# A fused Mamba, attention and expert kernel: query and key split into bfloat16 parts on TensorE and ScalarE instead of VectorE and ScalarE

## What is computed

```
x = x + mamba(group_norm(x))        # 256 inner channels, 16 states, 32 time steps
t = t + relu(attention(layer_norm(t)) @ proj_w + proj_b)
      attention: 8 heads of 16 channels over 800 tokens,
      softmax(q k^T * 128**-0.5) v, queries and keys kept at float32 precision
t = t + layer_norm(experts(layer_norm(t)) + layer_norm(t)) * gamma + beta    # top 2 of 8, per sample
```

## Time and profile before

| | |
|---|---|
| median of 3 runs | 1722.59 us (1722.4 to 1724.98) |
| profiled execution, span from first to last instruction | 1723.2 us |
| PE busy | 1238.6 us (72%) |
| DVE busy | 1338.4 us (78%) |
| ACT busy | 1110.6 us (64%) |
| POOL busy | 701.9 us (41%) |
| mean granted TensorE clock | 0.833 of full speed |

### The profile page before, as it was taken

One profiled execution on the slowest core, in us unless ns is written; L12 is line 12 of the kernel. 1 busy time (PEld: TensorE's weight loads), 2 busy tenths in 40 slices (PEclk: granted clock), 3 DMA queues, 4 the chain that ended last, 5 costly groups with the idle time before them and its releaser, 6 DMA issues. The chain is left out here.

```text
span 1723.2 us, 22121 instructions
## 1 busy us (share of the span) xinstructions
PE 1238.6 (72%) x7264; PEld 550.1 (32%) x7264; DVE 1338.4 (78%) x2280; ACT 1110.6 (64%) x2041; POOL 701.9 (41%) x399
## 2 busy tenths in 40 slices
PE   5124588868887688777886888588848873884994
PEld 3001432243224322432243224332323232322683
DVE  4898789888988889788979997899778972602465
ACT  4332767777776778677967686769676863682430
POOL 3464245524562356235623562346333641000265
PEclk9556788977898889878996899689968996896997
DMA  2540534145414641372228131824063404001562
GB/s 65 174 138 29 190 70 155 38 154 135 154 33 151 144 144 39 128 171 99 85 67 228 61 127 42 209 88 144 18 183 79 164 20 84 32 1 38 163 182 70
DMA packets 94023, 185.11 MB, mean 107 GB/s; under 512 B 15512, under 2 KB 48564, under 8 KB 93908
## 3 DMA queue, kind: packets, MB, share of 16 engines
q1 hardware_dynamic: 92500, 180.41, 35.2%
q0 software_dynamic: 1408, 3.29, 0.6%
HBM read 146.47 MB, written 36.86 MB: 106 GB/s over the span
## 5 line engine op out<-in xcount | busy, mean ns | idle before, releaser
L1274 DVE TENSOR_TENSOR_SCAN hst<-dA,PS 128x800 f32<-128x800 f32 x256 | 466.2, 1821 | 38.5 <-ACT dA L939 5.6
L1001 ACT ACTIVATE probs<-PS 128x400 f32<-128x400 f32 x800 | 343.0, 533 | 61.7 <-PE PS L1573 61.6
L939 ACT ACTIVATE dA<-dt_rep,a_sb 128x775 f32<-128x775 f32 x256 | 244.7, 959 | 78.6 <-DVE hst L1274 53.4
L1573 PE MATMUL PS<-q_stack,k_stack 99*128 99x400 bf16 (+1 forms) x896 | 238.5, 356 | 76.8 <-ACT probs L1001 51.0
L1269 DVE TENSOR_TENSOR PS<-u_rep,b_rep 128x800 f32<-128x800 f32 x256 | 267.6, 1045 | 14.1 <-DMA u_rep<-u_dram 2.3
L991 ACT ACTIVATE probs<-PS 128x400 f32<-128x400 f32 x400 | 200.4, 503 | 107.6 <-PE PS L1540 90.3
L1294 DVE CUSTOM_DVE_ANT_0 probs<-PS,probs 128x400 f32<-128x400 f32 x400 | 220.4, 574 | 41.6 <-issue 29.0
L796 POOL TENSOR_TENSOR sp_l<-hst,c_rep 128x800 f32<-128x800 f32 x72 | 135.6, 1883 | 196.2 <-DVE PS L1269 196.1
L1558 PE MATMUL PS<-probs,v_ext 128*32 128x400 f32 (+1 forms) x1792 | 206.9, 540 | 5.6 <-ACT probs L1001 5.6
L796 POOL TENSOR_TENSOR dt_sb<-hst,c_rep 128x800 f32<-128x800 f32 x72 | 135.7, 1884 | 110.8 <-DVE PS L1269 78.5
L1539 PE MATMUL PS<-k_stack,q_stack 96*128 96x400 bf16 (+1 forms) x448 | 152.0, 375 | 39.9 <-DVE k_neg L1253 37.5
(11 more groups left out here) (225 smaller groups left out, 2110.0 us busy)
## 6 DMA issues: line engine op xcount, KB each, us to landing
b_rep<-b_dram SPq DMA_DIRECT2D x64, 400.0 KB, 4.4
c_rep<-c_dram SPq DMA_DIRECT2D x64, 400.0 KB, 4.0
dt_rep<-dt_dram SPq DMA_DIRECT2D x64, 400.0 KB, 6.4
u_rep<-u_dram SPq DMA_DIRECT2D x64, 400.0 KB, 6.5
q_stack<-parts_dram SPq DMA_DIRECT2D x96, 100.0 KB, 4.3
k_stack<-parts_dram SPq DMA_DIRECT2D x96, 100.0 KB, 5.3
dt_dram<-dt_sb SPq DMA_DIRECT2D x16, 400.0 KB, 3.4
u_dram<-sp_l SPq DMA_DIRECT2D x16, 400.0 KB, 3.8
```

The source lines that it names most:

```text
L939: nc.scalar.activation(dA[:, i % NDA, :].rearrange("p (j t) -> p j t", t=T)[:, :, 1:T], dt_rep[:, gi, :].rearrange("p (j t) -> p j t", t=T ...
L1001: nc.scalar.activation(probs[:, j % NPROB, :], bank(4 + j % 3, HALF), ACT.Exp, scale=ATT_SCALE).then_inc(probs_ready.sem, 1)
L1274: nc.vector.tensor_tensor_scan(hst[:, i % 2, :], dA[:, i % NDA, :], dbu, 0.0, ALU.mult, ALU.add).then_inc(scan_done.sem, 1)
L1573: last = nc.tensor.matmul(bank(4 + j % 3, HALF)[strip], k_stack[:, h, kt * P:kt * P + strip.stop - strip.start], q_stack[:, h, q0:q0 + HAL ...
```

## The change

- **The split.** q and k stay in PSUM. ScalarE rounds what is there to a bfloat16 part; TensorE multiplies the part by a negated identity and accumulates onto the same PSUM banks, so that the remainder stands there; this is done twice, and ScalarE rounds three times for q and three times for k (before: two each, and VectorE did the four subtractions). The exponential of the Mamba half now runs ahead of the first rounding.
- **Negated keys.** The k projection uses a negated weight for the tokens 0 to 399. So k_stack holds the first 400 keys negated, k_neg and its two VectorE instructions per sample are gone, and TensorE waits for the stacks themselves. The first-half scores come out negated, so the maximum now subtracts them from the Relu, with the operands in the other order.
- **Signs.** The exponential's scale is negative for key tiles 0 to 2, positive for 4 to 6, and for key tile 3, which has both kinds of keys, a value per partition read from SBUF. The rows of ones in k_stack are -1 for the first half.
- **The step ahead of a maximum** (`tile_seen`) is gone: the waits stand directly before the maximum.
- At the start a negated weight (w_k_neg), a negated identity and the scale tile are made, and TensorE waits for the first of these before its first projection.

```diff
@@ -451,6 +451,11 @@
+        def unit_scale(i):
+
+            kt = unit(i)[1]
+            return (-ATT_SCALE if (kt + 1) * P <= HALF else ATT_SCALE if kt * P >= HALF else score_scale[:, 0:1])
+
         def group_of(i):
@@ -745,7 +750,10 @@
                 pool_order.after(pool, 0, nc.gpsimd.memset(v_ext[:, :, :, :], 1.0))
-                nc.gpsimd.memset(k_stack[KST:KST + 3, :, :], 1.0).then_inc(pads_set, 1)
+                pool_order.after(pool, 0, nc.gpsimd.memset(score_scale[:, :], ATT_SCALE))
+                pool_order.after(pool, 0, nc.gpsimd.memset(score_scale[0:HALF % P, :], -ATT_SCALE))
+                pool_order.after(pool, 0, nc.gpsimd.memset(k_stack[KST:KST + 3, :, 0:HALF], -1.0))
+                nc.gpsimd.memset(k_stack[KST:KST + 3, :, HALF:TOK], 1.0).then_inc(pads_set, 1)
                 pool.wait_ge(pads_set, 1)
@@ -962,15 +970,20 @@
                         if i == LOW_AT:
-                            act.wait_ge(q_up.sem, q_up.at(n, 1))
-                            nc.scalar.copy(q_part[:, 0, :], wide(4)).then_inc(qk_first.sem, 1)
                             if m is not None:
                                 exp_of(m, 1)
+                            act.wait_ge(q_up.sem, q_up.at(n, 1))
+                            nc.scalar.copy(q_part[:, 0, :], wide(4)).then_inc(qk_part.sem, 1)
                             act.wait_ge(k_up.sem, k_up.at(n, 1))
-                            nc.scalar.copy(k_part[:, 0, :], wide(6)).then_inc(qk_first.sem, 1)
-                            for i_part, (part, rest) in enumerate(((q_part, part_rest[:, :]), (k_part, sp_e[:, 0, :]))):
-                                act.wait_ge(qk_rest.sem, qk_rest.at(n, i_part + 1))
-                                nc.scalar.copy(part[:, 1, :], rest).then_inc(qk_second.sem, 1)
+                            nc.scalar.copy(k_part[:, 0, :], wide(6)).then_inc(qk_part.sem, 1)
+                            act.wait_ge(qk_rest.sem, qk_rest.at(n, 1))
+                            nc.scalar.copy(q_part[:, 1, :], wide(4)).then_inc(qk_part.sem, 1)
+                            act.wait_ge(qk_rest.sem, qk_rest.at(n, 2))
+                            nc.scalar.copy(k_part[:, 1, :], wide(6)).then_inc(qk_part.sem, 1)
+                            act.wait_ge(qk_rest.sem, qk_rest.at(n, 3))
+                            nc.scalar.copy(q_part[:, 2, :], wide(4)).then_inc(qk_parts.sem, 1)
+                            act.wait_ge(qk_rest.sem, qk_rest.at(n, 4))
+                            nc.scalar.copy(k_part[:, 2, :], wide(6)).then_inc(qk_parts.sem, 1)
                         if n > 0 and i == LOW_AT + 1:
@@ -999,7 +1012,7 @@
                             nc.scalar.activation(probs[:, j % NPROB, :], bank(4 + j % 3, HALF), ACT.Exp,
-                                                 scale=ATT_SCALE).then_inc(probs_ready.sem, 1)
+                                                 scale=unit_scale(j)).then_inc(probs_ready.sem, 1)
                             for acc in range(3):
@@ -1105,6 +1119,7 @@
                 dve.wait_ge(weights_in, NW[0])
+                nc.vector.tensor_scalar(w_k_neg[:, :], w_qkv_sb[:, C:2 * C], -1.0, None, ALU.mult).then_inc(w_k_turned, 1)
@@ -1236,26 +1251,7 @@
-                def rests():
-
-                    for i, (part, b, rest) in enumerate(((q_part, 4, part_rest[:, :]), (k_part, 6, sp_e[:, 0, :]))):
-                        dve.wait_ge(qk_first.sem, qk_first.at(n, i + 1))
-                        nc.vector.tensor_tensor(rest, wide(b), part[:, 0, :], ALU.subtract).then_inc(qk_rest.sem, 1)
-
-                def low_parts():
-
-                    for i, (part, rest) in enumerate(((q_part, part_rest[:, :]), (k_part, sp_e[:, 0, :]))):
-                        dve.wait_ge(qk_second.sem, qk_second.at(n, i + 1))
-                        nc.vector.tensor_tensor(part[:, 2, :], rest, part[:, 1, :], ALU.subtract).then_inc(qk_parts.sem, 1)
-
-                def negate_keys(half):
-                    dve.wait_ge(stacks_in[half].sem, stacks_in[half].at(n, 16 * NSTK))
-                    nc.vector.tensor_scalar(k_neg[:, 4 * half:4 * half + 4, :], k_stack[0:KST, 4 * half:4 * half + 4, 0:HALF],
-                                            -1.0, None, ALU.mult).then_inc(k_neg_ready.sem, 1)
-
                 for i in range(NSTEP):
-                    if n is not None and i == MAX_FROM:
-                        negate_keys(0)
                     if m is not None:
@@ -1281,18 +1277,12 @@
                     if n is not None:
-                        if i == LOW_AT:
-                            rests()
-                            low_parts()
                         for j in max_share(i):
                             _, _, found = max_item(j)
-                            if j == PER_ACC // 2:
-                                negate_keys(1)
                             dve.wait_ge(relu_ready.sem, relu_ready.at(n, j + 1))
                             dve.wait_ge(smax_up.sem, smax_up.at(n, j + 1))
-                            dve.sem_inc(tile_seen.sem, 1)
-                            nc.vector.tensor_tensor_reduce(probs[:, j % NPROB, :], bank(4 + 2 * (j % 2), HALF),
-                                                           probs[:, j % NPROB, :], 1.0, LOWEST, ALU.add, ALU.max,
+                            nc.vector.tensor_tensor_reduce(probs[:, j % NPROB, :], probs[:, j % NPROB, :],
+                                                           bank(4 + 2 * (j % 2), HALF), 1.0, LOWEST, ALU.subtract, ALU.max,
                                                            found).then_inc(smax_read.sem, 1)
@@ -1394,11 +1384,11 @@
-            def over_spans(b, lhsT, rhs, start=True, stop=True):
+            def over_spans(b, lhsT, rhs, start=True, onto=False):
                 for at, width in SPANS:
                     last = nc.tensor.matmul(PS[:, b * BANK + at:b * BANK + at + width], lhsT, rhs[:, at:at + width],
-                                            start=start, stop=stop)
+                                            start=start, stop=True, skip_group_check=onto)
                 return last
@@ -1532,12 +1523,13 @@
                         if k % PER_ACC == 0:
-                            pe.wait_ge(k_neg_ready.sem, k_neg_ready.at(n, k // PER_ACC + 1))
+                            half = k // PER_ACC
+                            pe.wait_ge(stacks_in[half].sem, stacks_in[half].at(n, 16 * NSTK))
                         if k >= 2:
                             pe.wait_ge(relu_ready.sem, relu_ready.at(n, k - 1))
                         for strip, h, q in queries(k):
                             nc.tensor.matmul(bank(5 + 2 * (k % 2), HALF)[strip], q, k_stack[0:KST, h, HALF:TOK], start=True, stop=False)
-                            last = nc.tensor.matmul(bank(5 + 2 * (k % 2), HALF)[strip], q, k_neg[:, h, :], start=False, stop=True)
+                            last = nc.tensor.matmul(bank(5 + 2 * (k % 2), HALF)[strip], q, k_stack[0:KST, h, 0:HALF], start=False, stop=True)
                         last.then_inc(diff_up.sem, 1)
@@ -1582,7 +1574,15 @@
                     over_spans(4, w_qkv_sb[:, 0:C], lnT).then_inc(q_up.sem, 1)
-                    over_spans(6, w_qkv_sb[:, C:2 * C], lnT).then_inc(k_up.sem, 1)
+                    for lo, hi in ((0, HALF), (HALF, BANK), (BANK, TOK)):
+                        last = nc.tensor.matmul(PS[:, 6 * BANK + lo:6 * BANK + hi], w_k_neg[:, :] if lo < HALF else w_qkv_sb[:, C:2 * C],
+                                                lnT[:, lo:hi], start=(lo % BANK == 0), stop=True,
+                                                skip_group_check=(lo % BANK > 0))
+                    last.then_inc(k_up.sem, 1)
+                    for a in range(2):
+                        for i_part, (part, b) in enumerate(((q_part, 4), (k_part, 6))):
+                            pe.wait_ge(qk_part.sem, qk_part.at(n, 2 * a + i_part + 1))
+                            over_spans(b, neg_ident_bf[:, :], part[:, a, :], start=False, onto=True).then_inc(qk_rest.sem, 1)
                     pe.wait_ge(qk_parts.sem, qk_parts.at(n, 1))
...
```

14 lines of the change are left out of this document (8 added, 6 removed).

## The result

| | before | after |
|---|---|---|
| median (runs) | 1722.2 us (8) | 1716.25 us (8) |
| lowest to highest | 1718.22 to 1724.98 | 1711.32 to 1719.02 |
| profiled execution: its time, its span, mean granted clock | 1724.98, 1723.2, 0.833 | 1715.6, 1713.9, 0.850 |

The ratio is 0.9971, with a 95% interval of 0.9957 to 0.9985. A later repeat of the same two kernels gave 1715.89 us (12 runs) against 1720.89 us (17 runs), 0.9968 [0.9956, 0.998]. So the change gains 5 to 6 us. That is faster by more than the measurement's 0.2%, and inside the range that was given, at half of the forecast gain. Every ratio in this document is to runs of before taken beside that kernel; medians of different experiments are compared by these ratios.

The account below looks back on a forecast made before the run. ScalarE and TensorE, not VectorE (busiest at 78%), were taken to end a sample's steps. Gains 3.4 + 3.4 + 11.5 = 18.3 us less losses of 7.4 gave 10.9 us less, 1712 us; range 1695 to 1727.

Parts of the forecast that it names:

- The maxima start when the stacks land: Start of each sample's maxima: TensorE waits for the stacks' DMA directly, not for the negation; 3.4 us gained in all.
- the parts: Splitting q and k: the new chain of roundings and subtractions ends 0.4 us later a sample, bounds 0.2 and 0.8.
- ScalarE's queue: ScalarE behind the split: added roundings and waits stay covered before the first Relu, with 0.4 us of cover left.
- The exponential's scale: Softmax: 16 of 100 exponentials a sample read their scale from SBUF; 7.4 us lost, bounds 3.2 and 11.6.
- The step ahead of the maximum: Maxima at the fast clock: the increment between wait and maximum costs 0.15 us; removing it gains 11.5 us.
- the delay belongs to the maximum: Rival, chance 0.22: the 0.18 us are the maximum's own start, the loop stays 1.16 us; 1.8 us slower, 1724 us.
- ScalarE's loop at 0.55: Maxima at the fast clock: ScalarE's Relu loop, 1.10 us for two tiles, sets the pace once the increment is gone.
- The slow distances taken as equal: Maxima at the slow clock: the number of slow distances stays; each one more or less is 0.4 us.
- the negation: Among the maxima: the second negation goes, 0.98 us becomes a normal 0.55 us distance; 3.4 us gained in all.
- VectorE's work off the end: Rival, chance 0.05: the VectorE work removed comes off the total; 41.7 us faster, 1681 us.

Follow-up runs that it names:

- experiment 1: The kernel before without the increment ahead of each maximum: 1717.02 us, 0.9965 of before.
- experiment 2: The kernel after with the increment put back ahead of each maximum: 1717.98 us, 0.9975 of before.
- experiment 5: The kernel after without the wait for the Relu ahead of each maximum, except for the last two tiles: 1710.16 us, 0.9919 of before.
- experiment 6: The kernel before without the increment, and with the wait for the Relu only for the last two tiles: 1710.16 us, 0.9923 of before.
- experiment 7: The kernel after with the two waits swapped, first for the scores, then for the Relu: 1709.63 us, 0.9932 of before.
- experiment 4: The kernel after with a plain subtraction in place of the maximum, so no maximum is found: 1719.1 us in one execution.
- experiment 8: The kernel after with the old split of q and k: VectorE subtracts, exponential behind q's first rounding: 1711.36 us, 0.9934 of before.
- experiment 3: The kernel after with a constant scale in all exponentials, the sign of 16 keys wrong: 1715.71 us, 0.9962 of before.
- experiment 10: The kernel after with one wait, the 16 mixed keys turned by VectorE and constant scales in all exponentials: 1713.29 us, 0.9943 of before.
- experiment 9: The kernel after with the old split (VectorE subtracts) and one wait ahead of a maximum: 1709.92 us, 0.9937 of before.

## Why the prediction was right or wrong, step by step

- **The maxima start when the stacks land:** right. TensorE's first difference waits for the DMA (3.21 us), and VectorE 2.89 us for its first scores. Gain 3.5 us against 3.4, with other parts: the store to the first difference is 6.0 shorter (5.4), the parts 2.8 later (3.2), and ahead of the first maximum 0.3 instead of 1.2, since the increment costs so little. The lower bound of this term is mis-summed in the prediction: 8 x (0.68 + 0.15 - 0.8 - 0.4) is -3.0 us, not -3.2.
- **ScalarE's queue:** right; the first Relu follows TensorE's first difference by 0.87 us (0.85 in the earlier trace rows).
- **The exponential's scale:** right in size, 7.6 us against 7.4; how it comes about is worked out in the prediction from a share of ScalarE's time, and only the sum was tested.
- **The step ahead of the maximum: this step failed.** "I put the 0.15 us to the increment that stands between wait and maximum." The delay was real and its size right, but the step took the increment for all that stands there. Experiments 1 and 2 give the increment 0.03 us. Experiments 5, 6 and 7 give 0.115 us to the wait for the scores, which is written last and is an instruction of its own, and which the change leaves in place. The loop of two tiles is therefore 1.13 us and not 1.01, still longer than ScalarE's 1.10, and the term about 320 x 0.012 = 3.8 us, not 11.5. The comparison behind the step was unfair: the plain instruction of the earlier trace rows, within 0.02 us of TensorE, has one signal to wait for, and the maximum has two; it carries its wait itself, like the maximum of experiment 5. The rival "the delay belongs to the maximum" is wrong as well (experiment 4 still has 0.65 of 0.68 us, experiment 5 has the same maximum at 0.37), but for this change its loop (no gain) is nearer to the 3.8 us than the forecast's.
- **ScalarE's loop at 0.55:** right, once the other loop is out of the way: 0.544 in experiment 4, 0.555 in experiment 5.
- **The slow distances taken as equal:** not so. Two profiles of after have 63 and 67, two of before 66 and 54 (without the negations). Five more on average, at 0.40 us, are 2.0 us. With 3.4 for the negation and 3.8 for the loop this is the 5.2 us of the table. How many are slow varies between executions of one kernel by more than that, so I don't put it to the change.
- **VectorE's work off the end:** this rival is wrong, as held; experiment 8 puts the subtractions back for nothing.

Two stages moved that had no term. From the last maximum to the first exponential it is 1.5 us more. From the last exponential to the next projections it is 4.2 us less: over the first five samples this stage is 45.45 us everywhere in the two profiles of after, while four of the ten of before are at 47.0; in the sixth sample it is 46.1 in both of after and 47.7 in both of before. These six make 4.7 us a profile. But neither belongs to the change: experiment 6, which is before with two lines altered, has no 47.0; experiment 1, before with one line less, has neither 47.0 nor 47.7; and experiment 4, built on after, has the 47.7. Why is open.

With 3.8 in place of 11.5, and 0.9 less for the first maxima, the prediction's own sum is 3.4 - 0.9 + 3.4 + 3.8 - 7.4 = 2.3 us gained. The table's stages sum to 3.8: the start of the maxima gave 1.0 us more than the 2.5 of this sum, the slow distances took 2.0, the scale took 0.2 more, and the two stages with no term gave 4.2 - 1.5 = 2.7. From there to the 5 to 6 us of the medians (with an interval from 2.6 to 7.4 in the first comparison) the sum is not closed: 1.2 to 2.2 us are left, well under the 6 us by which two profiles of one kernel differ.

The Trainium skill, "VectorE: DVE Perf Modes", section "The DRAIN you can't avoid", found that a semaphore after each of eight instructions added no time. The increment's 0.03 us lies close to it. The 0.115 us of a wait ahead of the maximum is another case, in which a signal is really waited for; there the measurement decides, and the order of the waits counted.

**What stays open.** Experiments 3, 10 and 9 each shorten stages by 2 to 6.6 us without the total following. In 3 a part is given back by the projections, more of which ran at the slow clock. Whether it is always the clock that takes the gain wasn't settled, nor what the split on TensorE costs beyond its 2.2 us. No experiment gave a plain instruction one wait in this loop, and why an instruction that holds only a wait costs 0.115 us is not shown. The lowest ratios have the kernels of experiments 5, 6 and 7, at 0.992 to 0.993; those of 8 to 10 lie within their intervals. These three beat both kernels, and the one with the smallest edit is the kernel before with one line out and one wait made rare.

## What to carry to other kernels

Before a delay is put to the one instruction that looks special, look in the trace for what would stand between signal and work without it, and compare with a place that has the same number of waits. Write the wait for the signal that comes last first, or drop the wait that is implied; in this loop the delay so removed was 0.115 us, four times that of the increment. And hold a shortened stage against the total time: here 6.6 us less in one stage were 0.5 us in the median.

## What the runs showed of the hardware

- Two waits ahead of one VectorE instruction: with the late signal in the wait written last, the start came 0.48 us behind the start of TensorE's last matmul (0.33 us long); with the order swapped, or with one wait, 0.37 us. The wait written last is an instruction of its own in the trace (EVENT_SEMAPHORE). An increment of the engine itself between wait and instruction: 0.03 us more. At the slow clock the three are 0.717 (with the increment), 0.687 and 0.578 us.
- A plain subtraction with two waits in the old order starts 0.44 us behind, or 0.65 at the slow clock. With one wait it wasn't run.
- A scale per partition makes a 128x400 exponential 607 ns instead of 533 on average, and 16 of 100 of them made the softmax stages 7.6 us longer over eight samples.
- Runs of one kernel spread by 5 to 15 us. Its profiles differ in the number of slow distances (66 and 54 in before) and in the projections: k's 288 columns took 430 and 478 ns in the mean of the two profiles of after, and 654 in that of experiment 3, with the same work there.
